# Last attention: odd heads' scores in the general banks, and one quarter of the down products a head

## The chip, the cores and the metric

One core of a Trainium2 chip runs the whole program. The metric is device time in microseconds (us), the median of several executions. TensorE does the matmuls, VectorE and ScalarE read and write PSUM (8 banks of 128 x 512 float32), GpSimd works on SBUF only, and SyncE issues the DMAs.

## The reference

The program is one transformer layer on x of 8 batches x 512 tokens x 512 features, in float32:

```python
x = x + _layernorm(attn(_layernorm(x), w_attn, b_attn, w_proj, b_proj))
x = x + _layernorm(ffn(_layernorm(x), w_fc, w_proj))

# attn: 16 heads of 32 features, rotary factors by head index
q, k, v = split(x @ w_attn + b_attn)
attn = softmax(where(causal, q @ k.T, -inf), axis=-1) * E ** -0.5
return (attn @ v) @ w_proj + b_proj
# ffn: both layers have ternary weights sign(round(w / mean|w|)) * mean|w|
# and a layer norm on their input (512 -> 2048 -> 512)
return bitlinear(gelu(bitlinear(x, w_fc)), w_proj)
```

## The kernel before

The work is staged as a software pipeline over the batches. Iteration `j` does the feed-forward part of batch j-1 (`prev`), the attention of batch j (`here`) and the projections to queries, keys and values of batch j+1 (`nxt`). With 8 batches the iterations run from -1 to 8, and iteration 7 is the one in which `prev` and `here` hold and `nxt` does not: the last attention. Iteration 8 has only the feed-forward part of batch 7. Each engine's program is written out by hand in order, with semaphores between them; there is no scheduler.

A float32 value is carried as a pair of float16 values, high and low. ScalarE writes the high half (`HI`) from a PSUM bank and leaves the whole value there, and VectorE subtracts the two (`low`, L950) to get the low half (`LO`). So every bank passes TensorE, ScalarE and VectorE before it is free.

The 8 PSUM banks are three `score` banks, three `gen` banks (general), `pv` and `down`. The general banks are handed out in a fixed order (`general_plan`), each use waiting for the third use before it to be drained (`claim`, semaphore `g_drained`); the score banks have a list of their own (`score_plan`, `claim_score`, `s_drained`). A head's scores fill three banks in parts of 512, 512 and 256 columns (`SCORE_W`).

After the 16 `up` products (L488) with their GELU, an iteration goes through its head loop. For head h TensorE issues the quarters of the down products that `DOWN_AT` lists for h (`ffn_down`, L531, 8 matmuls a quarter, 4 quarters for each tile of 128 tokens), then `scores(h + 1)` (a mask matmul, L563, and seven products, L557), then `weigh(h)`, the 20 products of probabilities and values (L585), which waits for all three subtractions of head h and for `pv` to be read out. In head 0 the quarter comes behind `weigh(0)`. The four quarters of tile 0 are done before the loop. ScalarE takes the exponentials of head h+1 (two per part, L809 and L811), and in heads 6, 9 and 13 a final normalisation of a tile (`FINISH_AT`, L816). VectorE subtracts for head h+1 (`probs_low`, L950), then reads out head h (`head_output`: reciprocal L1199, reduction L1201, product into xo L1206); in the heads of `FINAL_AT` it also drains the bank `down` of a tile (`final`, L1151) ahead of the subtractions and takes the moments (`final_moments`, L1157) behind them, and in head 6 the variance of the hidden layer, which waits for that head's weighing. GpSimd sums the squares of the hidden layer in the meantime (L1446, L1448, L1451), and head 6's `square_sums` on TensorE (L519) needs its last add. SyncE issues the stores of finished tiles, and in this iteration, behind the store of tile 2 and the last quarter, the load of the residual (L407).

Of the kernel before, what the change touches and what calls it, by code (L numbers as in the profile page):

```python
# [26 lines left out]
BATCHES, T, E, HEADS = 8, 512, 512, 16  # L27
HD = E // HEADS
F = 4 * E
PARTS = 128  # L30
# [10 lines left out]
S_UP = W_UP * W_UP  # L41
# [20 lines left out]
           13: [(3, 0), (3, 1)], 14: [(3, 2), (3, 3)]}  # L62
FINAL_AT = {8: 1, 12: 2}
SQUARES_AT = 6
FINISH_AT = {6: 0, 9: 1, 13: 2}
# [18 lines left out]


def general_plan(prev, here, nxt, setup):

    uses = []
    for u in range(FC):
        uses += [("shift", 0)] if here and u == SHIFT_AT else []  # L90
        uses += [("up", u)] if prev else []
        uses += [("xT", X_AT[u])] if nxt and u in X_AT else []
    if nxt and not here:
        uses += [("v", tb) for tb in range(TB)]
    for h in range(HEADS):
        uses += [("qk", QK_AT[h])] if nxt and h in QK_AT else []
        uses += [("next max", 3 * STEP_MAX[h] + i) for i in range(3)] if here and nxt and h in STEP_MAX else []
    if here:
        for name, n in (("v", 0), ("oT", 0), ("oT", 1), ("oT", 2), ("oT", 3), ("v", 1), ("x2T", 0), ("v", 2), ("x2T", 1), ("v", 3),
                        ("x2T", 2), ("x2T", 3)):  # L100
            if name != "v" or nxt:
                uses.append((name, n))
    return {name: k for k, name in enumerate(uses)}
# [9 lines left out]
def score_plan(here, nxt):  # L113

    uses = [("max", h) for h in range(EARLY, HEADS)] + [("scores", 0)] if here else []
    for h in range(HEADS):
        if here and h + 1 < HEADS:
            uses.append(("scores", h + 1))
    if nxt and not here:
        uses += [("next max", h) for h in range(EARLY)]  # L120
    return {use: 3 * k for k, use in enumerate(uses)}
# [31 lines left out]
def build(nc, x, w_attn, b_attn, b_v, w_proj, b_proj, w_fc, w_down, rope, out):  # L153
# [4 lines left out]
    HI, LO = 0, 1  # L158
# [4 lines left out]
    with ExitStack() as ctx:  # L163
# [256 lines left out]
        def _(pe):  # L420
# [41 lines left out]
            def iteration(j, prev, here, nxt, setup):  # L462
# [91 lines left out]
                def scores(h):  # L554
# [4 lines left out]
                    if h == 0:  # L559
                        pe.wait_ge(k_rows, 16)  # L560
                        pe.wait_ge(shift_rows, 32 * (j + 1))
                    bank = claim_score(("scores", h), 0)
                    nc.tensor.matmul(bank[:, :].rearrange("p (b t) -> p b t", b=TB), identb[:, :],  # L563
                                     mask_b[:, :].unsqueeze(1).to_broadcast([PARTS, TB, PARTS]),
                                     start=True, stop=False, skip_group_check=True)
                    for s in range(TB):
                        mm = part(bank, PARTS * s, s, PARTS * s, PARTS * (s + 1), False)
                    mm.then_inc(s_full, 1)
                    bank = claim_score(("scores", h), 1)
                    part(bank, 0, 0, PARTS, T, True)  # L570
                    part(bank, 384, 2, 3 * PARTS, T, False).then_inc(s_full, 1)
                    bank = claim_score(("scores", h), 2)
                    part(bank, 0, 1, 2 * PARTS, T, True).then_inc(s_full, 1)

                def weigh(h):

                    pe.wait_ge(s_drained, s0 + S["scores", h] + 3)
                    need(pe, pv_drained, HEADS * j + h)
# [44 lines left out]
                def project(tb):  # L623
# [3 lines left out]
                    if tb < 3:  # L627
                        pe.wait_ge(s_drained, s0 + S["scores", HEADS - 1] + tb + 1)
                    else:
                        pe.wait_ge(pv_drained, HEADS * (j + 1))  # L630
# [53 lines left out]
                for h in range(HEADS):  # L684
# [8 lines left out]
                    if nxt and not here and h == 5:  # L693
                        value_bias_projected()
                    pieces = DOWN_AT.get(h, ()) if prev else ()
                    if h:
# [51 lines left out]
        def _(act):  # L748
# [6 lines left out]
            def iteration(j, prev, here, nxt, setup):  # L755
# [49 lines left out]
                def exponents(h):  # L805

                    for i, n in enumerate(SCORE_W):
                        act.wait_ge(s_full, s0 + S["scores", h] + i + 1)
                        nc.scalar.activation(probs[:, h % 2, HI, 512 * i:512 * i + n], score[i][:, 0:n], ACT.Exp,  # L809
                                             scale=1.0 / S_UP)  # L810
                        nc.scalar.activation(score[i][:, 0:n], score[i][:, 0:n], ACT.Exp, scale=1.0 / S_UP  # L811
                                             ).then_inc(exp_full, 1)
# [132 lines left out]
        def _(dve):  # L945
# [69 lines left out]
            def iteration(j, prev, here, nxt, setup):  # L1015
# [170 lines left out]
                def probs_low(h):  # L1186

                    for i, n in enumerate(SCORE_W):
                        dve.wait_ge(exp_full, 48 * j + 3 * h + i + 1)
                        at = 512 * i  # L1190
                        low(probs[:, h % 2, LO, at:at + n], score[i][:, 0:n], probs[:, h % 2, HI, at:at + n]
                            ).then_inc(s_drained, 1)

# [78 lines left out]
                if nxt and not here:  # L1272
# [13 lines left out]
                    v_low(TB - 1)  # L1286
                    bias_ready()
                for h in range(HEADS):
                    if setup and h == 2:
# [9 lines left out]
                    if nxt and not here and h == 6:  # L1299
                        projection_bias()  # L1300
                    if prev and h in FINAL_AT:
                        final(FINAL_AT[h])
                    if prev and here and h == SQUARES_AT:
                        hidden_variance()
                        final_terms(0)
                    if here:
# [4 lines left out]
                        head_output(h)  # L1311
                    if prev and h in FINAL_AT:
                        final_moments(FINAL_AT[h])
                        final_terms(FINAL_AT[h])
                    if setup and h == 2:
# [214 lines left out]
```

## Time and profile before

| | us |
|---|---|
| median of 3 runs (range) | 1337.46 (1334.47 to 1338.87) |
| the profiled execution: its time | 1333.62 |
| its span, first to last instruction | 1331.8 |
| TensorE matmuls busy in the span | 1192.1 (90%) |
| VectorE / ScalarE / GpSimd busy | 1019.6 / 769.0 / 593.6 |
| last attention's head loop | 1165.2 to 1230.7 |

"Busy" counts the time of an engine's own operations; PE is TensorE's matmul, PEld its weight load, DVE is VectorE, ACT ScalarE, POOL GpSimd, SPq SyncE's DMA queue. "Idle before" and the name behind the arrow in brackets say how long an engine waited ahead of an operation and what ended the wait. PEclk is the clock granted to TensorE, 1.00 for 2.4 GHz and 0.50 for 1.2 GHz. Successive operations of one engine overlap in the records, so a pace is read from start to start. L12 is line 12 of the kernel. Head h of the last attention is known by its place: scores of head 0 stand ahead of the loop, those of head 1 at 1168.76 us.

### The profile page before, as it was taken

The numbers are of one execution on the slowest core, as the hardware profiler recorded it, in microseconds if no ns is written. First come the engines' busy times: TensorE is split into PE (matmuls) and PEld (weight loads), VectorE is DVE, ScalarE is ACT, GpSimd is POOL, SyncE is SP. The second block draws the span as 40 slices with busy tenths as digits, with TensorE's granted clock in tenths as the row PEclk, the third lists the DMA queues.
The fourth block names the chain that finished last, engine by engine and source line by source line (L and its number), as shares of the span: only waits on it lengthen the run. The fifth ranks groups of instructions, "written<-read, shape, count | busy, mean of one in ns | idle before, by whom it ended". The sixth has DMA issues, their size and how long they took to land.

```text
span 1331.8 us, 24946 instructions
## 1 busy us (share of the span) xinstructions
PE 1192.1 (90%) x9364; PEld 648.4 (49%) x9364; DVE 1019.6 (77%) x2931; ACT 769.0 (58%) x1414; POOL 593.6 (45%) x636
## 2 busy tenths in 40 slices
PE   4755879999999999999999999999999999988796
PEld 2322545455545554455545554455545554554352
DVE  7588896878878797978788787968787887776532
ACT  3334874666556664666556754666466755576470
POOL 6131441692049502791159412871259313971252
PEclk9865898999999999999999999999999999999798
DMA  5451122002310113002300213002300221001000
GB/s 205 132 154 62 38 70 57 1 2 57 96 40 3 39 51 103 1 8 67 89 32 2 57 43 94 1 18 70 106 1 3 57 78 27 2 9 48 9 1 32
DMA packets 49825, 65.37 MB, mean 49 GB/s; under 512 B 8581, under 2 KB 33189, under 8 KB 49192
## 3 DMA queue, kind: packets, MB, share of 16 engines
q1 hardware_dynamic: 49704, 63.77, 16.5%
q8 instruction: 74, 1.21, 0.4%
q14 instruction: 47, 0.39, 0.1%
HBM read 29.89 MB, written 8.39 MB: 29 GB/s over the span
## 4 chain that ended last, share of the span: by engine, by line
PE 51%; DVE 33%; ACT 8%; POOL 3%; issue 3%; SPq 1%; DMA 1%; POOLq 0%; DVEq 0%; ACTq 0%
PE gen L488 18%; PE down L531 17%; DVE score L1089 9%; PE pv L585 4%; DVE hT L950 4%; PE score L557 4%; DVE probs L950 2%; DVE acc_add L1066 2%; PE score L563 2%; DVE mx L1089 1%; DVE qkn L1181 1%; POOL rstd L1422 1%; DVE bn L1118 1%; ACT qkn L753 1%; PE gen L548 1%
## 5 line engine op out<-in xcount | busy, mean ns | idle before, releaser
L1422 POOL TENSOR_TENSOR rstd<-veps,mhalf 128x1 f32<-128x1 f32 (+1 forms) x104 | 67.5, 649 | 472.5 <-DVE veps L1166 363.9
L809 ACT ACTIVATE probs<-score 128x512 f16<-128x512 f32 (+1 forms) x384 | 202.4, 527 | 122.1 <-PE score L557 122.1
L950 DVE TENSOR_TENSOR probs<-score,probs 128x512 f16<-128x512 f32 (+1 forms) x384 | 213.4, 597 | 61.2 <-ACT score L811 60.8
L488 PE MATMUL gen<-x2T,t1T 128*128 128x512 f16 x1024 | 242.6, 382 | 4.0 <-ACT x2T L752 2.5
L531 PE MATMUL down<-t2T,hT 128*128 128x512 f16 x1024 | 234.1, 381 | 3.5 <-DVE xn L1151 3.5
L811 ACT ACTIVATE score<-score 128x512 f32<-128x512 f32 (+1 forms) x384 | 205.4, 535 | 0.0
L488 PE MATMUL gen<-xT,wa 128*128 128x512 f16 x768 | 178.6, 383 | 12.2 <-DVE wa L970 8.4
L950 DVE TENSOR_TENSOR hT<-gen,hT 128x512 f16<-128x512 f32 x160 | 108.9, 687 | 65.8 <-ACT gen L772 27.6
L1089 DVE CUSTOM_DVE_ANT_0 score<-score,mask_rows 128x512 f32<-128x512 f32 (+1 forms) x344 | 158.0, 523 | 0.0
L531 PEld LDWEIGHTS down<-t2T,hT 128*128 128x128 f16 x1024 | 96.7, 98 | 111.3 <-DVE xn L1151 4.7
L488 PEld LDWEIGHTS gen<-x2T,t1T 128*128 128x128 f16 x1024 | 95.4, 98 | 109.4 <-ACT x2T L752 5.2
L771 ACT ACTIVATE hT<-gen,gam 128x512 f16<-128x512 f32 x128 | 88.3, 690 | 95.5 <-PE gen L488 95.4
L1451 POOL TENSOR_TENSOR acc<-acc,acc_add 128x512 f32<-128x512 f32 x105 | 133.1, 1268 | 8.2
L1446 POOL TENSOR_TENSOR acc_add<-hT 128x512 f32<-128x512 f16 x105 | 121.3, 1155 | 14.8 <-POOL acc L1451 0.9
L488 PEld LDWEIGHTS gen<-xT,wa 128*128 128x128 f16 x768 | 72.1, 99 | 94.9 <-DVE wa L970 8.9
L1448 POOL TENSOR_TENSOR acc_add<-acc_add 128x512 f32<-128x512 f32 x105 | 109.4, 1041 | 8.2
L585 PE MATMUL pv<-v_sb,probs 128*128 128x65 f16 x2560 | 101.8, 196 | 5.5 <-DVE oA L1201 5.5
L585 PEld LDWEIGHTS pv<-v_sb,probs 128*128 128x128 f16 x2560 | 96.2, 99 | 12.5 <-DVE probs L950 6.9
L557 PE MATMUL score<-qk 98*128 98x128 f16 (+2 forms) x896 | 98.3, 247 | 1.4 <-DVE probs L950 1.4
L488 PE MATMUL gen<-wa,xT 128*128 128x512 f16 x384 | 90.3, 387 | 3.8 <-DVE wa L976 3.8
L753 ACT ACTIVATE qkn<-gen,qk_bias 128x512 f16<-128x512 f32 x64 | 44.1, 689 | 83.8 <-PE gen L488 73.7
L557 PEld LDWEIGHTS score<-qk 98*128 98x128 f16 x896 | 68.2, 99 | 43.0 <-DVE probs L950 7.0
(136 smaller groups left out, 1838.3 us busy)
## 6 DMA issues: line engine op xcount, KB each, us to landing
qk<-qkn SPq DMA_DIRECT2D x384, 64.0 KB, 2.0
xo<-x SPq DMA_DIRECT2D x8, 1024.0 KB, 5.6
hT<-x SPq DMA_DIRECT2D x8, 1024.0 KB, 6.3
out<-xn SPq DMA_DIRECT2D x32, 256.0 KB, 2.2
hT<-w_fc SPq DMA_DIRECT2D x4, 1024.0 KB, 6.4
hT<-w_down SPq DMA_DIRECT2D x4, 1024.0 KB, 5.5
hT<-w_attn SPq DMA_DIRECT2D x4, 512.0 KB, 10.0
hT<-w_attn SPq DMA_DIRECT2D x1, 1024.0 KB, 8.7
```

The lines of the kernel that those rows point to most:

```text
L488: mm = nc.tensor.matmul(bank[:, :], a, b, start=(start and n == 0), stop=(stop and n == len(pairs) - 1))
L531: mm = nc.tensor.matmul(down[:, :], hT[:, half, u, PARTS * tb:PARTS * (tb + 1)], t2T[:, u, :], start=(u == 0 and half == HI), stop=(u == F ...
L557: return nc.tensor.matmul(bank[:, at:at + t1 - t0], qk[0:98, 1, h, PARTS * s:PARTS * (s + 1)], qk[0:98, 0, h, t0:t1], start=start, stop=Tr ...
L585: mm = nc.tensor.matmul(pv[:, VW * tb:VW * (tb + 1)], probs[:, h % 2, half, at:at + PARTS], v_sb[:, s, h, :], start=(s == 0 and half == HI ...
L771: nc.scalar.activation(hT[:, HI, u, :], bank[:, :], ACT.Gelu, scale=gam[:, 0:1])
L809: nc.scalar.activation(probs[:, h % 2, HI, 512 * i:512 * i + n], score[i][:, 0:n], ACT.Exp, scale=1.0 / S_UP)
L811: nc.scalar.activation(score[i][:, 0:n], score[i][:, 0:n], ACT.Exp, scale=1.0 / S_UP).then_inc(exp_full, 1)
L950: return V.tensor_tensor(out, whole, hi, ALU.subtract)
L1089: op = V.tensor_tensor_reduce(part, part, mask_rows[:, T - n:T], 1.0, -3.0e38, ALU.add, ALU.max, mx[:, TB * u + tb:TB * u + tb + 1])
L1446: P.tensor_tensor(whole[:, :], hT[:, HI, u, :], hT[:, LO, u, :], ALU.add).then_inc(sq_step, 1)
L1448: P.tensor_tensor(whole[:, :], whole[:, :], whole[:, :], ALU.mult).then_inc(sq_step, 1 if u else 2)
L1451: P.tensor_tensor(acc[:, :], acc[:, :], acc_add[:, :], ALU.add).then_inc(sq_step, 1)
```

## The change

In the iteration without `nxt` the scores of odd heads go to the general banks (`scores_in_general`): the general plan gets three more uses for each odd head, the score plan loses them, and the waits and signals of TensorE, ScalarE and VectorE follow. The quarters of tiles 1 to 3 move from pairs in few heads to one in each of the heads 0, 1, 2, 4, 7, 8, 9, 10, 12, 13, 14 and 15 (`LAST_DOWN_AT`), and VectorE's finals of tiles 1 and 2 from heads 8 and 12 to heads 6 and 11. ScalarE's `FINISH_AT` stays. All other iterations are as they were.

```diff
 DOWN_AT = {0: [(1, 0)], 5: [(1, 1), (1, 2)], 6: [(1, 3)], 9: [(2, 0), (2, 1)], 10: [(2, 2), (2, 3)],
            13: [(3, 0), (3, 1)], 14: [(3, 2), (3, 3)]}
 FINAL_AT = {8: 1, 12: 2}
+LAST_DOWN_AT = {h: [divmod(n + 4, 4)] for n, h in enumerate((0, 1, 2, 4, 7, 8, 9, 10, 12, 13, 14, 15))}
+LAST_FINAL_AT = {6: 1, 11: 2}
...
+def scores_in_general(h, nxt):
+    return not nxt and h % 2 == 1 and h < HEADS
...
     for h in range(HEADS):
...
+        uses += [("scores", 3 * (h + 1) + i) for i in range(3)] if here and not nxt and scores_in_general(h + 1, nxt) else []
...
-        if here and h + 1 < HEADS:
+        if here and h + 1 < HEADS and not scores_in_general(h + 1, nxt):
             uses.append(("scores", h + 1))
...
+                    in_general = scores_in_general(h, nxt)
+                    full = g_full if in_general else s_full
+                    def claim_part(i):
+                        return claim("scores", 3 * h + i) if in_general else claim_score(("scores", h), i)
-                    bank = claim_score(("scores", h), 0)
+                    bank = claim_part(0)
...
-                    pe.wait_ge(s_drained, s0 + S["scores", h] + 3)
+                    if scores_in_general(h, nxt):
+                        drained("scores", 3 * h + 2)
+                    else:
+                        pe.wait_ge(s_drained, s0 + S["scores", h] + 3)
...
-                        pe.wait_ge(s_drained, s0 + S["scores", HEADS - 1] + tb + 1)
+                        pe.wait_ge(s_drained, s0 + S["scores", HEADS - 1 if nxt else HEADS - 2] + tb + 1)
...
-                    pieces = DOWN_AT.get(h, ()) if prev else ()
+                    pieces = (DOWN_AT if nxt or not here else LAST_DOWN_AT).get(h, ()) if prev else ()
...
-                        act.wait_ge(s_full, s0 + S["scores", h] + i + 1)
+                        if scores_in_general(h, nxt):
+                            bank = filled("scores", 3 * h + i)
+                        else:
+                            act.wait_ge(s_full, s0 + S["scores", h] + i + 1)
+                            bank = score[i]
...
-                        low(probs[:, h % 2, LO, at:at + n], score[i][:, 0:n], probs[:, h % 2, HI, at:at + n]
-                            ).then_inc(s_drained, 1)
+                        bank = bank_of("scores", 3 * h + i) if in_general else score[i]
+                        low(probs[:, h % 2, LO, at:at + n], bank[:, 0:n], probs[:, h % 2, HI, at:at + n]
+                            ).then_inc(g_drained if in_general else s_drained, 1)
...
+                final_at = FINAL_AT if nxt or not here else LAST_FINAL_AT
...
-                    if prev and h in FINAL_AT:
-                        final(FINAL_AT[h])
+                    if prev and h in final_at:
+                        final(final_at[h])
```

On TensorE, heads 4 and 5 of the last attention, before, from the weighing of head 3 to the scores of head 6:

```order
L585 MATMUL pv<-v_sb,probs 128x65 x20
L563 MATMUL score<-mask_b,identb 128x512
L557 MATMUL score<-qk 128x128 x4
L557 MATMUL score<-qk 128x384
L557 MATMUL score<-qk 128x128
L557 MATMUL score<-qk 128x256
L585 MATMUL pv<-v_sb,probs 128x65 x20
L531 MATMUL down<-t2T,hT 128x512 x16
L563 MATMUL score<-mask_b,identb 128x512
```

The same place after the change (the lines of the kernel have moved by 8 to 17):

```order
L602 MATMUL pv<-v_sb,probs 128x65 x20
L539 MATMUL down<-t2T,hT 128x512 x8
L577 MATMUL gen<-mask_b,identb 128x512
L565 MATMUL gen<-qk 128x128 x4
L565 MATMUL gen<-qk 128x384
L565 MATMUL gen<-qk 128x128
L565 MATMUL gen<-qk 128x256
L602 MATMUL pv<-v_sb,probs 128x65 x20
L577 MATMUL score<-mask_b,identb 128x512
```

The two quarters (16 matmuls) between the weighing of head 4 and the scores of head 6 are gone from there, one quarter (8) stands ahead of the scores of head 5, and those scores are in the general banks.

At the end of the loop on TensorE, before, from the scores of head 14 on:

```order
L563 MATMUL score<-mask_b,identb 128x512
L557 MATMUL score<-qk 128x128 x4
L557 MATMUL score<-qk 128x384
L557 MATMUL score<-qk 128x128
L557 MATMUL score<-qk 128x256
L585 MATMUL pv<-v_sb,probs 128x65 x20
L531 MATMUL down<-t2T,hT 128x512 x16
L563 MATMUL score<-mask_b,identb 128x512
L557 MATMUL score<-qk 128x128 x4
L557 MATMUL score<-qk 128x384
L557 MATMUL score<-qk 128x128
L557 MATMUL score<-qk 128x256
```

After that the old program has the weighings of heads 14 and 15 in one row (`x40`). The new one, from the scores of head 15 on:

```order
L577 MATMUL gen<-mask_b,identb 128x512
L565 MATMUL gen<-qk 128x128 x4
L565 MATMUL gen<-qk 128x384
L565 MATMUL gen<-qk 128x128
L565 MATMUL gen<-qk 128x256
L602 MATMUL pv<-v_sb,probs 128x65 x20
L539 MATMUL down<-t2T,hT 128x512 x8
L602 MATMUL pv<-v_sb,probs 128x65 x20
```

The last quarter has moved in between the weighings of heads 14 and 15.

On VectorE in head 6, from the output of head 5 on, before:

```order
L1206 TENSOR_TENSOR xo<-oA,r_sum 128x4x32
L1138 TENSOR_TENSOR h_msq<-h_negm 128x4
L1140 SCALAR_TENSOR_TENSOR h_var<-pv,h_msq 128x4
L1143 TENSOR_SCALAR e_fin<-h_var,c_fin 128x4
L1166 TENSOR_TENSOR veps<-mv,e_fin 128x1
L950 TENSOR_TENSOR probs<-score,probs 128x512 x2
```

And now:

```order
L1229 TENSOR_TENSOR xo<-oA,r_sum 128x4x32
L1172 SCALAR_TENSOR_TENSOR xn<-c_sum,h_negm,down 128x512
L1159 TENSOR_TENSOR h_msq<-h_negm 128x4
L1161 SCALAR_TENSOR_TENSOR h_var<-pv,h_msq 128x4
L1164 TENSOR_SCALAR e_fin<-h_var,c_fin 128x4
L1187 TENSOR_TENSOR veps<-mv,e_fin 128x1
L971 TENSOR_TENSOR probs<-gen,probs 128x512 x2
```

The final of tile 1 (`xn<-c_sum,h_negm,down`) now stands ahead of the variance, and its moments follow behind the output of head 6.

## Rows read from the trace of the kernel before

**Rows 1.** view in windows of the head loop; first line names the columns
```profile
core 0: us, PE busy (x) PEld busy (x) DVE busy (x) ACT busy (x) POOL busy (x), PEclk, DMA share, GB/s
...
1165.20:1230.70 65.50, 53.67 (x564) 32.30 (x562) 47.59 (x114) 44.64 (x99) 27.73 (x28) 0.95 0.09 29
...
1172.50:1181.30 8.80, 5.74 (x84) 3.51 (x82) 7.85 (x18) 7.84 (x19) 8.06 (x8) 1.00 0.01 2
...
1190.00:1193.90 3.90, 2.22 (x35) 1.75 (x32) 2.30 (x10) 2.67 (x6) 0.55 (x1) 0.97 0.00 0
...
1187.10:1204.20 17.10, 14.96 (x146) 9.70 (x145) 12.61 (x33) 11.45 (x25) 4.28 (x7) 0.80 0.05 17
```

**Rows 2.** waits in the head loop: us in total, times, longest
```profile
ACT probs L809 <- PE score L557: 18.7, 11, 3.4
```

**Rows 3.** timeline of ScalarE: start us, us, engine, line, out<-in, idle before
```profile
1169.40 0.60 ACT L809 ACTIVATE probs<-score 128x512 f16<-128x512 f32 x1 [1.56 <-PE score L557]
...
1172.50 0.60 ACT L809 ACTIVATE probs<-score 128x512 f16<-128x512 f32 x1 [0.44 <-PE score L557]
...
1175.08 0.61 ACT L809 ACTIVATE probs<-score 128x512 f16<-128x512 f32 x1
...
1187.09 0.60 ACT L809 ACTIVATE probs<-score 128x512 f16<-128x512 f32 x1 [3.13 <-PE score L557]
...
1222.97 0.81 ACT L816 ACTIVATE xn<-xn,shift,rstd 128x512 f32<-128x512 f32 x1
...
1225.22 0.60 ACT L809 ACTIVATE probs<-score 128x512 f16<-128x512 f32 x1 [1.44 <-PE score L557]
```

**Rows 4.** timeline of TensorE, heads 0 to 2
```profile
1168.76 0.38 PE L563 MATMUL score<-mask_b,identb 128*128 128x512 bf16 x1
...
1169.53 0.77 PE L585 MATMUL pv<-v_sb,probs 128*128 128x65 f16 x20
...
1170.13 1.89 PE L531 MATMUL down<-t2T,hT 128*128 128x512 f16 x8
...
1171.86 0.38 PE L563 MATMUL score<-mask_b,identb 128*128 128x512 bf16 x1
...
1174.37 0.39 PE L563 MATMUL score<-mask_b,identb 128*128 128x512 bf16 x1 [0.51 <-DVE probs L950]
```

**Rows 5.** timeline of VectorE and TensorE at the last head
```profile
1227.35 1.02 DVE L950 TENSOR_TENSOR probs<-score,probs 128x512 f16<-128x512 f32 x2 [0.31 <-ACT score L811]
...
1228.91 0.78 PE L585 MATMUL pv<-v_sb,probs 128*128 128x65 f16 x20 [2.80 <-DVE oA L1201]
```

**Rows 6.** timeline of VectorE: the product of a head, beside GpSimd and alone
```profile
1176.15 1.25 DVE L1206 TENSOR_TENSOR xo<-oA,r_sum 128x128 f32<-128x128 f32 x1
...
1182.35 0.29 DVE L1206 TENSOR_TENSOR xo<-oA,r_sum 128x128 f32<-128x128 f32 x1
```

**Rows 7.** timeline: weighing of heads 6 and 7, statistics of tile 1
```profile
1191.62 0.76 PE L585 MATMUL pv<-v_sb,probs 128*128 128x65 f16 x20
...
1195.36 1.31 PE L585 MATMUL pv<-v_sb,probs 128*128 128x65 f16 x20
...
1202.07 0.68 DVE L1157 BATCH_NORM_STATS2 bn<-xn 128x6 f32<-128x512 f32 x1
```

**Rows 8.** timeline of TensorE: weighing of head 12, then tile 3's first quarters
```profile
1215.32 0.76 PE L585 MATMUL pv<-v_sb,probs 128*128 128x65 f16 x20 [0.21 <-DVE oA L1201]
...
1216.29 3.63 PE L531 MATMUL down<-t2T,hT 128*128 128x512 f16 x16 [0.21 <-DVE xn L1151]
```

**Rows 9.** timeline of GpSimd: its last sum of squares
```profile
1187.44 1.27 POOL L1451 TENSOR_TENSOR acc<-acc,acc_add 128x512 f32<-128x512 f32 x1
```

**Rows 10.** timeline of TensorE: products of the first and the second projection
```profile
1232.37 3.89 PE L488 MATMUL score<-wp,hT 128*128 128x512 f16 x12
...
1236.74 2.75 PE L488 MATMUL score<-wp,hT 128*128 128x512 f16 x12
```

**Rows 11.** DMA issues of the page: KB each, median us to landing
```profile
hT<-x SPq DMA_DIRECT2D x8, 1024.0 KB, 6.3
```

More of the change, by code:

```diff
@@ L567, in scores @@
                         mm = part(bank, PARTS * s, s, PARTS * s, PARTS * (s + 1), False)
-                    mm.then_inc(s_full, 1)
-                    bank = claim_score(("scores", h), 1)
+                    mm.then_inc(full, 1)
+                    bank = claim_part(1)
                     part(bank, 0, 0, PARTS, T, True)
-                    part(bank, 384, 2, 3 * PARTS, T, False).then_inc(s_full, 1)
-                    bank = claim_score(("scores", h), 2)
-                    part(bank, 0, 1, 2 * PARTS, T, True).then_inc(s_full, 1)
+                    part(bank, 384, 2, 3 * PARTS, T, False).then_inc(full, 1)
+                    bank = claim_part(2)
+                    part(bank, 0, 1, 2 * PARTS, T, True).then_inc(full, 1)
                 def weigh(h):
-                    pe.wait_ge(s_drained, s0 + S["scores", h] + 3)
+                    if scores_in_general(h, nxt):
+                        drained("scores", 3 * h + 2)
+                    else:
+                        pe.wait_ge(s_drained, s0 + S["scores", h] + 3)
                     need(pe, pv_drained, HEADS * j + h)
@@ L807, in exponents @@
                     for i, n in enumerate(SCORE_W):
-                        act.wait_ge(s_full, s0 + S["scores", h] + i + 1)
-                        nc.scalar.activation(probs[:, h % 2, HI, 512 * i:512 * i + n], score[i][:, 0:n], ACT.Exp,
+                        if scores_in_general(h, nxt):
[3 more added lines that the diff above has]
+                            bank = score[i]
+                        nc.scalar.activation(probs[:, h % 2, HI, 512 * i:512 * i + n], bank[:, 0:n], ACT.Exp,
                                              scale=1.0 / S_UP)
-                        nc.scalar.activation(score[i][:, 0:n], score[i][:, 0:n], ACT.Exp, scale=1.0 / S_UP
+                        nc.scalar.activation(bank[:, 0:n], bank[:, 0:n], ACT.Exp, scale=1.0 / S_UP
                                              ).then_inc(exp_full, 1)
@@ L1190, in probs_low @@
                         at = 512 * i
-                        low(probs[:, h % 2, LO, at:at + n], score[i][:, 0:n], probs[:, h % 2, HI, at:at + n]
-                            ).then_inc(s_drained, 1)
+                        in_general = scores_in_general(h, nxt)
+                        bank = bank_of("scores", 3 * h + i) if in_general else score[i]
+                        low(probs[:, h % 2, LO, at:at + n], bank[:, 0:n], probs[:, h % 2, HI, at:at + n]
+                            ).then_inc(g_drained if in_general else s_drained, 1)
                 def head_output(h):
@@ L1311, in iteration @@
                         head_output(h)
-                    if prev and h in FINAL_AT:
-                        final_moments(FINAL_AT[h])
-                        final_terms(FINAL_AT[h])
+                    if prev and h in final_at:
+                        final_moments(final_at[h])
+                        final_terms(final_at[h])
                     if setup and h == 2:
```

## The prediction

> **What bounds the kernel now.** I read the page first, then the stretch of the last attention in windows, the list of waits there, the chain of waits, and the timeline of that stretch engine by engine. Nothing before 1165 us changes, since both edits are switched by "no next batch", so only the 65.5 us of the last attention's head loop [rows 1] and what follows it can move. In that stretch TensorE is busy 53.67 us, VectorE 47.59, ScalarE 44.64: none is full, so it is a question of how they wait for each other. The longest sum of waits on the working engines is ScalarE's for score matmuls, 18.7 us [rows 2].
>
> The reader is to see three paces there. I call M(h) the start of head h's mask matmul, E(h) the start of its first exponential, W(h) the start of its weighing matmuls. (a) ScalarE's own pace: E(2) to E(3) is 1172.50 to 1175.08, 2.58 us a head with no wait between [rows 3]. (b) TensorE's pace with one down quarter in the head: M(1) at 1168.76, W(0) at 1169.53, the quarter at 1170.13, M(2) at 1171.86 [rows 4]: 0.77 + 0.60 + 1.73 = 3.10. (c) Two quarters in one head make it 3.10 + 1.73 = 4.83, and ScalarE then stands idle: 3.13 us ahead of E(6) at 1187.09 [rows 3]. So the heads without a quarter run at ScalarE's pace while TensorE idles (5.74 of 8.80 us busy in 1172.5 to 1181.3 [rows 1]), and those with two at TensorE's pace while ScalarE idles. The 14 head gaps from E(1) at 1169.40 to E(15) at 1225.22 make 55.8; at ScalarE's pace they would be 14 x 2.58 + 3 finals x 0.8 [rows 3] = 38.5. The other 17.3 and the 1.56 ahead of E(1) are the 18.7 of [rows 2].
>
> **The change part by part.** Work: the same matmuls, exponentials and subtractions, on other banks and in another order. Nothing is added or removed but waits.
>
> The spread of the quarters is the term that pays. The constants for the new order come from rows: M to E 0.64 (1168.76 to 1169.40 [rows 3, 4]); M to W at least 0.77, W to the next matmul 0.60, a quarter 1.73 [rows 4]; E to W 3.69 where nothing else stands on VectorE (1225.22 to 1228.91, the three subtractions and then the reduction of the head before [rows 3, 5]); a final on ScalarE 0.8 [rows 3]. In the new order M(h+1) follows W(h-1) + 0.60 + the quarter; a wait for a bank is never last, because head h+1 uses the banks of head h-1, whose subtractions end before W(h-1) begins. So M(h+1) = W(h-1) + 0.60 + 1.73 q; E(h) = the later of M(h) + 0.64 and E(h-1) + 2.58; W(h) = the later of E(h) + 3.69 and M(h+1) + 0.77. Up to W(0) = 1169.53 and E(1) = 1169.40 nothing moves (M(1) waits for the last half of tile 0, not for a bank).
>
> Head by head, in us after 1165: two quarters lie between W(0) and M(2) (those of heads 0 and 1): M(2) 8.6, E(2) 9.2, W(1) 9.4. Quarter of head 2: M(3) 11.7, E(3) 12.3, W(2) 12.9. None: M(4) 13.5, E(4) 14.9, W(3) 16.0. Quarter: M(5) 18.4, E(5) 19.0, W(4) 19.1. Two heads with none: E(6) 21.6, W(5) 22.7, M(7) 23.3, E(7) 24.2, W(6) 25.3. Here sits a detour that stays: the variance waits for head 6's weighing, and W(7) comes 3.74 after W(6) (1191.62 to 1195.36 [rows 7]); new W(7) = 29.0. M(8) 27.6, and ScalarE's final of tile 0 holds E(8) to 28.6. VectorE's moments of tile 1, now done ahead of head 8's subtractions, cost some 1.3 (0.68 for the statistics [rows 7], and three short steps), on top of a 1.25 product, so W(8) is 33.3 and not 32.3. Then four quarters in a row: M(9) 31.4, E(9) 32.0; M(10) 35.7, E(10) 36.3, W(9) 36.5; M(11) 38.8, E(11) 39.7 behind a final, W(10) 40.0; M(12) 40.6, E(12) 42.3, W(11) 43.4. Tile 3's first quarter waits for the final on VectorE, which starts after head 10's output: it started 0.97 after a weighing (1215.32 to 1216.29 [rows 8]) and does so again, at 44.4: M(13) 46.1, E(13) 46.7, W(12) 46.9. M(14) 49.2, E(14) 49.8, W(13) 50.4; M(15) 52.8, E(15) 53.4, W(14) 53.5; W(15) = E(15) + 3.69 = 57.1. The last quarter, now in head 15, ends at 53.5 + 2.33 = 55.8, so it is hidden by 1.3 us behind that wait; without the cover it would cost 1.73. Before, W(15) was at 63.9 [rows 5]. Gain 6.8.
>
> The banks by themselves: in the old scheme M(h+1) also waits for head h's first subtraction, E(h) + 1.87 (1172.50 to M(3) at 1174.37 [rows 3, 4]), and with M to E 0.64 that gives E(h+1) = E(h) + 2.51, no more than ScalarE's own 2.58. So they pay only where VectorE is late with that subtraction: after a slow product (below), at the variance, and at the finals in heads 6 and 11. I put 1 to 2 of the 6.8 on them, and nothing on the fixed cost of another bank, since the same engines read general banks of the same size all through the kernel; from the nearest rows this is 0 on both sides.
>
> What I subtract: VectorE's product of a head takes 0.29 us, but 1.25 where GpSimd's sum of squares runs beside it [rows 6]. GpSimd works without a break until 1188.71 [rows 9], so heads 1 to 6 meet it. Of the five such products before it ended, one paid the full 0.96 and the others 0 to 0.3, mean about 0.3; they delay W only where E + 3.69 decides, heads 2, 3, 5 and 6. Bounds 0 and 4 x 0.96 = 3.8; I take 0.8, nearer the low end, because most of the observed ones were short. The specification table of the Trainium skill's "GPSIMD Engine Reference" ("Specifications") says that GpSimd shares its SBUF interfaces with VectorE, with contention for instructions with two SBUF inputs. By that rule every such product could pay, and the sum would go to the 3.8 end, a gain of 3.0; the rows show the 1.25 once in five, so the trace agrees on the mechanism and not on its being always paid.
>
> The squares' sums ahead of W(6) need GpSimd's last add. New, they can start at 24.2 (M(7) + 0.77 + 0.16), and that add ended at 23.7 [rows 9]: covered by 0.5 us only. If GpSimd is a microsecond later, 0.5 is lost there.
>
> The tail (from W(15) on) moves as it is. The residual's load waits for the last quarter, which now ends at 55.8, that is 1220.8, and lands 6.3 later [rows 11], at 1227.1. Its first reader comes behind the first projection, 1236.3 before [rows 10] and 1229.5 or later now, so it stays hidden, by 2.4 us at least. The clock of TensorE is the unknown. It was at 1.00 (2.4 GHz) in heads 2 to 5, and fell to the other level (1.2 GHz) behind a stretch with 2.22 of 3.90 us busy: a mean of 0.80 over 17.10 us means 6.8 us at half speed [rows 1]. It fell again for the first projection, whose 12 matmuls took 3.89 against 2.75 in the next [rows 10]. My sum takes full speed in the loop and the same tail. Bounds: if the tail's fall goes, +1.1; if a fall lands on the four quarters in a row, as long a one, 6.8 us, costs at most the 3.4 us of full-speed work that doesn't fit into it.
>
> Sum: 6.8 - 0.8 = 6.0 us. Against the profiled execution, 1333.62 (span 1331.8), that is 1327.6. The median of the three runs is 1337.46, 3.8 above the profiled one, so the forecast for the median is 1337.46 - 6.0 = 1331.5.
>
> **The rivals.** First, the clock falls in the new order as well and meets heads 7 to 10, which all hold a quarter. For it: heads 5 and 6 have no quarter and my times give TensorE 0.77 + 0.60 + 0.77 + 1.02 = 3.2 of 5.6 us, the same share as where it fell. Against: the quarters around them are fuller than before. Price 3.4: gain 2.6, 1334.9.
> Second, the shared port: each of the four products pays 0.96. For it [rows 6], against it the other four of five. Gain 6.8 - 3.8 = 3.0, 1334.5.
> Third, larger: no fall in the loop and none at the first projection, since TensorE now idles 1.3 us and not 2.8 ahead of W(15) [rows 5]; the slow-port loss also stays out. Gain 6.8 + 1.1 = 7.9, 1329.6.
> Fourth, slower: the clock falls twice in the loop (after heads 3 to 4 and after 5 to 6) and stays low into the start of the last up products. Against it: the old order had a sparser stretch, 1172.5 to 1181.3, at full clock throughout [rows 1]. Each fall costs up to 3.4, three of them 10.2, against a gain of 6.0: 1341.7. It decides from the second fall on, at which the gain is used up.
> That the change does not do what it says would be a second bank set that still waits for the first. It can't here: each wait for a general bank is three uses back, which is the same part of the head two before. What can be empty is its use, as the 2.51 against 2.58 above says, and that is in the sum.
>
> **How the numbers follow.** Forecast 0.55, clock on the quarters 0.17, port 0.09, larger 0.12, slower 0.07. A difference under 0.3%, 4.0 us, can't be told from no change in this kernel. Of the forecast's 0.55, whose own range is a gain of 4 to 8, I give 0.51 to above 4.0 and 0.04 below; the larger case adds 0.12: faster 0.63. The two small gains and the 0.04 make same 0.30, slower 0.07. The range leaves out the slower case and the far end of the larger: gain 0.5 to 9.5 with the runs' own scatter of some 2 us inside, 1328 to 1337.
>
> **What would show it.** E(15) about 49 us after E(1) in place of 55.8; no ScalarE wait for scores over 1.5 us after head 2 (3.13 and more before); W(h) to W(h+2) about 6.7 in the run of heads 8 to 10; the last quarter over before W(15); the granted clock at 1.00 through the loop; and W(15) near 1222. Wrong would be: W to W+2 longer than 7, GpSimd the one waited for at the squares' sums, or a loop shorter by 6 while the tail is longer by as much.

## The result and the profile after

| | before | after |
|---|---|---|
| median, 5 runs each (range), us | 1337.46 (1334.47 to 1339.36) | 1329.26 (1326.26 to 1331.13) |
| ratio, with its 95% interval | | 0.9937 (0.9915 to 0.9959) |
| profiled execution, its time / span | 1333.62 / 1331.8 | 1331.13 / 1329.3 |

Compared twice more, against new runs of before, the changed kernel stood at 0.9958 (0.9945 to 0.9971) and 0.9921 (0.9908 to 0.9935). So the gain is 5.6, 8.2 and 10.6 us in the three comparisons, where 6.0 was forecast.

The one profile shows 2.5 us of it. Splitting it at two points, the first mask matmul of the loop (head 0) and the last weighing, says why. The first rows are TensorE's timeline in the changed kernel: start us, us, engine, line, operation, and in brackets the idle time before it and what ended that.

```profile
1167.68 0.38 PE L577 MATMUL score<-mask_b,identb 128*128 128x512 bf16 x1
...
1172.67 0.77 PE L602 MATMUL pv<-v_sb,probs 128*128 128x65 f16 x20
...
1177.50 0.78 PE L602 MATMUL pv<-v_sb,probs 128*128 128x65 f16 x20
...
1181.06 0.76 PE L602 MATMUL pv<-v_sb,probs 128*128 128x65 f16 x20 [0.28 <-DVE oA L1224]
...
1184.17 1.18 PE L602 MATMUL pv<-v_sb,probs 128*128 128x65 f16 x20 [1.58 <-DVE oA L1224]
1185.16 3.15 PE L539 MATMUL down<-t2T,hT 128*128 128x512 f16 x8
...
1197.78 3.60 PE L539 MATMUL down<-t2T,hT 128*128 128x512 f16 x8
...
1215.54 0.77 PE L602 MATMUL pv<-v_sb,probs 128*128 128x65 f16 x20 [1.75 <-DVE oA L1224]
1216.50 1.90 PE L539 MATMUL down<-t2T,hT 128*128 128x512 f16 x8 [0.20 <-DVE xn L1172]
...
1226.27 1.89 PE L539 MATMUL down<-t2T,hT 128*128 128x512 f16 x8
1229.23 0.78 PE L602 MATMUL pv<-v_sb,probs 128*128 128x65 f16 x20 [1.06 <-DVE oA L1224]
...
1232.33 2.76 PE L496 MATMUL score<-wp,hT 128*128 128x512 f16 x12
```

The reader is to see four things. The loop starts at 1167.68, 3.1 us later than before (1164.54), in a part that is the same in both kernels. The weighings of heads 0 to 3 stand 5.0, 9.8, 13.4 and 16.5 us behind that start. Then two quarters take 3.15 and 3.60 us where the others take 1.9: TensorE was at the lower level of its clock (1.2 GHz) for most of each. And the last weighing comes 61.5 us after the start, 64.4 before ([rows 5], from 1164.54). The last quarter starts 2.96 us ahead of it and so is hidden, as said. Across the loop and at the two quarters, the windows say the same (time, then busy us of each engine, then PEclk):

```profile
1167.70:1229.20 61.50, 52.77 (x553) 32.21 (x550) 47.09 (x112) 44.39 (x99) 28.09 (x29) 0.92 0.04 14
```

```profile
1184.00:1188.00 4.00, 3.83 (x28) 2.06 (x29) 3.63 (x8) 1.72 (x5) 3.60 (x4) 0.57 0.00 0
1194.00:1201.50 7.50, 6.50 (x39) 4.15 (x39) 5.14 (x16) 3.42 (x8) 1.59 (x3) 0.54 0.00 0
```

ScalarE's waits for scores, in the list of waits of the changed kernel's loop, are two rows now, since odd heads read general banks:

```profile
ACT probs L830 <- PE gen L565: 7.5, 6, 3.1
ACT probs L830 <- PE score L565: 6.8, 5, 2.2
```

That is 14.3 us against 18.7 [rows 2]. Both hold the wait ahead of head 0's exponentials, 1.96 and 1.95 us; without it they are 12.3 and 16.7. Its timeline shows where the 3.1 is: behind the slow quarter of head 4. Further on the longest is 1.79 us.

```profile
1188.79 0.60 ACT L830 ACTIVATE probs<-gen 128x512 f16<-128x512 f32 x1 [3.07 <-PE gen L565]
...
1205.03 0.60 ACT L830 ACTIVATE probs<-gen 128x512 f16<-128x512 f32 x1 [0.45 <-PE gen L565]
...
1218.88 0.60 ACT L830 ACTIVATE probs<-gen 128x512 f16<-128x512 f32 x1 [1.79 <-PE gen L565]
...
1225.54 0.60 ACT L830 ACTIVATE probs<-gen 128x512 f16<-128x512 f32 x1 [0.18 <-PE gen L565]
```

From 1172.54 to 1225.54, E(1) to E(15) is 53.0 us, against 55.8 before and 49 forecast.

### The profile page after: what moved, and what is told of

Read it like the earlier page. It is cut to its first block, busy times and chain, and to the rows that moved or that the text cites. A ratio compares the mean times of both kernels' runs of the same rounds, so it can differ in the third digit from the quotient of the medians.

```text
span 1329.3 us, 24946 instructions
## 1 busy us (share of the span) xinstructions
PE 1192.4 (90%) x9364; PEld 649.2 (49%) x9364; DVE 1019.6 (77%) x2931; ACT 767.0 (58%) x1414; POOL 593.1 (45%) x636
## 4 chain that ended last, share of the span: by engine, by line
PE 50%; DVE 33%; ACT 9%; issue 3%; POOL 3%; SPq 1%; DMA 1%; POOLq 0%; DVEq 0%; ACTq 0%
PE gen L496 18%; PE down L539 16%; DVE score L1110 9%; PE pv L602 4%; DVE hT L971 4%; PE score L565 4%; DVE probs L971 2%; DVE acc_add L1087 2%; POOL rstd L1446 1%; DVE bn L1139 1%; PE score L577 1%; DVE mx L1110 1%; DVE qkn L1202 1%; ACT probs L830 1%; PE gen L556 1%
## 5 line engine op out<-in xcount | busy, mean ns | idle before, releaser
L830 ACT ACTIVATE probs<-score 128x512 f16<-128x512 f32 x360 | 189.5, 526 | 110.7 <-PE score L565 110.7
L971 DVE TENSOR_TENSOR probs<-score,probs 128x512 f16<-128x512 f32 x360 | 199.8, 596 | 53.2 <-ACT score L832 52.6
L832 ACT ACTIVATE score<-score 128x512 f32<-128x512 f32 x360 | 192.3, 534 | 0.0
L602 PE MATMUL pv<-v_sb,probs 128*128 128x65 f16 x2560 | 101.8, 196 | 9.4 <-DVE oA L1224 9.4
L602 PEld LDWEIGHTS pv<-v_sb,probs 128*128 128x128 f16 x2560 | 96.2, 99 | 17.6 <-DVE probs L971 13.4
L565 PE MATMUL score<-qk 98*128 98x128 f16 x840 | 90.2, 247 | 0.0
L1484 POOL TENSOR_SCALAR acc<-hT,theta 128x512 f16<-128x512 f32 x24 | 41.6, 1738 | 101.4 <-DVE g_sq L1063 76.2
```

The lines of the kernel that those rows point to most:

```text
L565: return nc.tensor.matmul(bank[:, at:at + t1 - t0], qk[0:98, 1, h, PARTS * s:PARTS * (s + 1)], qk[0:98, 0, h, t0:t1], start=start, stop=Tr ...
L602: mm = nc.tensor.matmul(pv[:, VW * tb:VW * (tb + 1)], probs[:, h % 2, half, at:at + PARTS], v_sb[:, s, h, :], start=(s == 0 and half == HI ...
L832: nc.scalar.activation(bank[:, 0:n], bank[:, 0:n], ACT.Exp, scale=1.0 / S_UP).then_inc(exp_full, 1)
L971: return V.tensor_tensor(out, whole, hi, ALU.subtract)
```

## The experiments

Each kernel with a ratio was compared with runs of before on the same chip at the same time; kernels measured together against the same runs of before are called a series. One series holds the banks alone, the spread alone, the changed kernel's second profile and the quarters in 0, 2, 4, 5; another holds the third profile and the last two kernels of the table; a third holds the old banks with those quarters, the short squares and the masks for 4, 6, 12. "Loop" is from head 0's mask matmul to the last weighing, "tail" from there to the end of the span, "start" the time of that mask matmul, all of the one profiled execution. Before and the spread alone were profiled once more and the changed kernel twice more, because one execution doesn't show how the clock falls in others.

| kernel | ratio (95%) | start | loop | clock in the loop | tail |
|---|---|---|---|---|---|
| before | 1 | 1164.5 | 64.4 | 0.95 | 102.9 |
| before, again | | 1167.6 | 65.2 | 0.92 | 102.0 |
| changed | 0.9937 (0.9915 to 0.9959) | 1167.7 | 61.5 | 0.92 | 100.1 |
| changed, second | 0.9958 (0.9945 to 0.9971) | 1165.8 | 61.6 | 0.92 | 101.2 |
| changed, third | 0.9921 (0.9908 to 0.9935) | 1164.2 | 60.5 | 0.94 | 100.2 |
| banks only | 0.9986 (0.9973 to 0.9998) | 1165.0 | 65.2 | 0.92 | 101.3 |
| spread only | 0.9946 (0.9931 to 0.9961) | 1164.3 | 58.7 | 1.00 | 101.9 |
| spread only, again | | 1164.8 | 58.7 | 1.00 | 101.8 |
| quarters 0, 2, 4, 5 | 0.9936 (0.9923 to 0.9949) | 1166.4 | 60.9 | 0.94 | 100.1 |
| the same, old banks | 0.9947 (0.9927 to 0.9967) | 1166.6 | 60.8 | 0.94 | 100.0 |
| changed, short squares | 0.9963 (0.9950 to 0.9976) | 1166.5 | 61.3 | 0.92 | 102.8 |
| changed, masks repeated for 4, 6, 12 | 0.9933 (0.9915 to 0.9951) | 1166.6 | 60.5 | 0.94 | 100.2 |
| changed, masks repeated for 7, 12 | 0.9926 (0.9913 to 0.9939) | 1168.1 | 59.9 | 0.97 | 101.8 |
| quarters 0, 2, 4, 5, masks for 4, 12 | 0.9914 (0.9901 to 0.9927) | 1165.2 | 57.9 | 0.97 | 103.0 |

**The banks alone.**

```diff
-LAST_DOWN_AT = {h: [divmod(n + 4, 4)] for n, h in enumerate((0, 1, 2, 4, 7, ...))}
-LAST_FINAL_AT = {6: 1, 11: 2}
+LAST_DOWN_AT = DOWN_AT
+LAST_FINAL_AT = FINAL_AT
```

> Only the banks change: odd heads' scores in the general banks, quarters and finals in their old heads. Theory A (the spread of the quarters pays, the banks hardly): by the rule of the prediction the old wait for a score bank allows a head every 2.51 us, under ScalarE's 2.58, so only VectorE's late subtractions are relieved: a gain of 0 to 2 us on before, with 3.1 us of ScalarE idle still ahead of heads 6 and 14. Theory B (the old bank wait was the stall): most of the change's 8 us is here, a gain of 6 to 8 us, and the spread alone brings under 2.

Measured: 0.9986, 1.9 us less than before, with its loop at 65.2 us. Theory B falls; the banks by themselves are worth 0.3 to 3.6 us by the interval, as theory A said. The loop of that profile is not shorter than before's. Its weighings run 0.5 to 0.6 us ahead of before's first profile from head 4 to head 8, but then two pairs of quarters take 4.49 and 4.46 us, where before's first profile has 4.00 and 3.63, because the clock was low for longer there. So the loop shows a small lead and not a gain.

**The spread alone.**

```diff
 def scores_in_general(h, nxt):
-    return not nxt and h % 2 == 1 and h < HEADS
+    return False
```

TensorE's wait for the last score banks behind the loop goes back to the one of before with it.

> Only the quarters and finals move; all scores stay in the score banks. Theory A: a gain of 5 to 8 us on before; the loop from head 0's mask matmul to the last weighing is 57 to 59 us where the clock stays up, against 64.4 before. Theory B: the spread quarters can't be used while every head waits for the bank of the head before: a gain under 2 us.

Measured: 0.9946, 7.2 us less, and loops of 58.7 us. That is all of the change's gain within the intervals; the changed kernel in the same series had 0.9958, so putting the general banks on top of the spread added nothing that can be seen. The row over the loop has the clock at 1.00:

```profile
1164.30:1223.00 58.70, 50.95 (x554) 29.90 (x551) 47.64 (x112) 44.50 (x99) 28.08 (x29) 1.00 0.04 15
```

> The kernel with only the quarters moved, once more, for its profile. Its first profile had no fall of the clock in the loop and 58.7 us from head 0's mask matmul to the last weighing. Theory C with falls that depend on where the execution stands: the loop is again 58.7 us if the clock stays up, and 60 to 63 us with one or two falls. If the order of work alone decided, it is 58.7 again.

It was the same to 0.01 us, with the clock up throughout, from a start 0.6 us later. Two starts so near each other don't tell whether the order alone decides or the start too. Both profiles are of quick executions, 1326.7 and 1327.2 us, where this kernel's timed runs go from 1326.1 to 1330.7; whether the clock falls in the loop of the longer ones is not known.

**The changed kernel again, and a third time.**

> The changed kernel itself, for one more profile of its loop. If the two falls of the clock seen in its first profile (15 us into the loop and 28 us into it) belong to the order of work, they are there again and the loop is 61 to 62 us. If they depend on where the execution happens to stand, they come elsewhere or not at all, and a loop without them is 57.6 us from head 0's mask matmul to the last weighing, as the prediction's head by head list has it. Time 1326 to 1332 us.

> The changed kernel a third time, on the chip of the two kernels with repeats, to compare with. Its falls at 26 and 46.5 us into the loop again (61.6 us), unless the loop starts elsewhere, as in the first profile, where they were at 16.6 and 26.9. Time 1327 to 1331 us.

The second profile had falls 26 and 46.5 us behind the start, and 61.6 us; the third, from the start of 1164.2, had only the one at 26, and 60.5; the first, above, had them at 16.6 and 27. So the third expectation was half right: no fall at 46.5, and a median just below the expected range (1326.75). Where the clock fell changed with the start of the loop within one order; that it fell in this order was so in all three.

**No two heads in a row without a quarter.**

```diff
-... enumerate((0, 1, 2, 4, 7, 8, 9, 10, 12, 13, 14, 15))}
+... enumerate((0, 2, 4, 5, 7, 8, 9, 10, 12, 13, 14, 15))}
```

> As the changed kernel, but tile 1's quarters in heads 0, 2, 4 and 5 and not 0, 1, 2 and 4: no two heads in a row without a quarter, and no double one ahead of head 2's scores. By the prediction's rules this is 0.8 us shorter at full clock. If sparse stretches in heads 3 and 5 to 6 are what lowers TensorE's clock, the falls become rarer and it gains 1 to 4 us on the changed kernel; if the falls don't follow the sparse heads, the two differ by under 1 us.

> All scores in the score banks, tile 1's quarters in heads 0, 2, 4 and 5. If the old bank wait costs next to nothing beside the spread (theory A), the same as the run with these heads and the general banks, 1327 us within 1.5. If the banks pay once no head pair is empty, 2 us or more slower than that.

Measured 0.9936 and, with old banks, 0.9947; loops of 60.9 and 60.8, both with falls 16 and 46.5 us behind the start and none at 26. The fall behind heads 5 and 6 went when head 5 got a quarter. Another came at 16, behind heads 1 and 3, of which head 1 had its quarter taken away. The start isn't the reason: the changed order with short squares starts at 1166.5 as well and has no fall at 16. With these heads the banks make no difference in the loop, as theory A has it; the ratios are 1.5 us apart, inside their intervals. Beside the 0.9936 the changed kernel had 0.9958, 2.9 us more, but 0.9937 and 0.9921 in its other two comparisons, so this order is not shown to be faster.

**Repeated mask matmuls.** The mask matmul starts the sum in its bank (start=True). Here it is issued several times into the same bank ahead of the scores; the extra ones change nothing in the result and only keep TensorE at work.

```diff
+                    for _ in range({4: 4, 6: 6, 12: 6}.get(h, 1) if not nxt else 1):
                         nc.tensor.matmul(bank[:, :]..., identb[:, :], mask_b..., start=True, stop=False, ...)
```

> The changed kernel with its mask matmul repeated into the same bank where TensorE has nothing else to do: 4 times for head 4, 6 times for heads 6 and 12 (each 0.216 us, start=True, so the result is the same). It adds 0.65 to 1.1 us of TensorE work to three sparse heads, inside slack by the prediction's rules (0.7, 1.2 and 1.2 us). Theory C (a sparse TensorE lowers the clock and that costs the loop 3 to 4 us): fewer falls in the loop, 1 to 4 us faster than the changed kernel. Rival (the falls don't depend on these heads): the same falls, 0 to 1 us slower.

The fall at 46.5 was gone, the one at 26 stayed, and the loop was 60.5: the third changed profile has the same without any repeats, from a start 2.3 us earlier. More telling are the three profiles without repeats for head 12 whose loops start within 0.2 us of this one's 1166.56: short squares and quarters 0, 2, 4, 5 with either banks. All three fell at 46.5, their quarters there taking 3.06, 3.54 and 3.56 us, and this one took 1.90. That is in favour of theory C, with one profile on its side. The time was 0.9933.

The next kernel has `{7: 4, 12: 6}` there.

> The changed kernel with the mask matmul repeated 4 times for head 7 and 6 times for head 12. With repeats for heads 4, 6 and 12 the fall at 46.5 us was gone and the one at 26 stayed. Theory C: head 7's scores stand right ahead of that fall, so it goes as well, and the loop is 58 to 59.5 us (0.5 us of the repeats can't be hidden there). Rival: the fall at 26 us belongs to the squares' sums and stays, the loop is 60.5 to 61.

Its loop started at 1168.1, near that of the first profile of the changed kernel (1167.7), which fell at 16.6 and at 27. It fell at 16.6 too, and not at 27. TensorE's timeline of that place, first of that profile of the changed kernel, then of this one:

```profile
1192.48 0.77 PE L602 MATMUL pv<-v_sb,probs 128*128 128x65 f16 x20 [2.03 <-DVE oA L1224]
1193.08 0.38 PE L577 MATMUL gen<-mask_b,identb 128*128 128x512 bf16 x1
1193.30 0.71 PE L565 MATMUL gen<-qk 98*128 98x128 f16 x7
1195.01 1.84 PE L527 MATMUL pv<-ones,acc 128*128 128x1 f32 x8 [1.00 <-DVE probs L971]
1196.71 1.26 PE L602 MATMUL pv<-v_sb,probs 128*128 128x65 f16 x20
1197.78 3.60 PE L539 MATMUL down<-t2T,hT 128*128 128x512 f16 x8
```

```profile
1192.89 0.77 PE L603 MATMUL pv<-v_sb,probs 128*128 128x65 f16 x20 [2.03 <-DVE oA L1225]
1193.50 1.02 PE L578 MATMUL gen<-mask_b,identb 128*128 128x512 bf16 x4
1194.36 0.71 PE L565 MATMUL gen<-qk 98*128 98x128 f16 x7
1195.43 1.02 PE L527 MATMUL pv<-ones,acc 128*128 128x1 f32 x8 [0.35 <-issue]
1196.31 0.76 PE L603 MATMUL pv<-v_sb,probs 128*128 128x65 f16 x20
1196.91 1.89 PE L539 MATMUL down<-t2T,hT 128*128 128x512 f16 x8
```

Three more mask matmuls in head 7, 0.65 us of work, and the squares' sums take 1.02 and not 1.84, the quarter 1.89 and not 3.60. All five profiles of this order without repeats for head 7 fell here, this one didn't, so theory C is supported for this fall, again by one profile. In time nothing is gained: 0.9926 beside 0.9921 for the changed kernel in the same series.

**Quarters in 0, 2, 4, 5 and masks repeated for heads 4 and 12.**

> General banks for odd heads, tile 1's quarters in heads 0, 2, 4 and 5, and the mask matmul repeated 6 times for heads 4 and 12, ahead of the two places where the clock fell in that order (15.8 and 46.5 us behind head 0's mask matmul). Theory C (sparse TensorE work lowers the clock, and work laid in there keeps it up): no fall in the loop, 57 to 58 us from head 0's mask matmul to the last weighing in place of 60.9, and 1 to 3 us faster than the same order without the repeats. Rival (falls come where they like): one or two falls at other places, no gain.

The loop was 57.9, as expected, though the clock did fall once, briefly, at 26, which was not expected. The falls at 16 and 46.5 were gone, but the loop started 1.3 us earlier than that of the same order without repeats, so what removed them is not shown. With 0.9914 it is the fastest kernel of the study, and it beats before by 11.5 us; its interval overlaps those of the other two kernels of its series, so against the changed kernel (0.9921) it is not shown to be faster. The tail was 103.0: against the changed kernel's third profile the loop is 2.6 us shorter and the tail 2.8 us longer, so in these two profiles the one makes up for the other.

**GpSimd's sums of squares shortened.** For all but the first of the 16 parts of the hidden layer, the three steps of the sum (the diff shows one) cover 8 of 512 columns in this iteration, so the squares of the other columns are left out of the variance.

```diff
+                    c = slice(0, T) if nxt or not u else slice(0, 8)
...
-                    P.tensor_tensor(whole[:, :], hT[:, HI, u, :], hT[:, LO, u, :], ALU.add)
+                    P.tensor_tensor(whole[:, c], hT[:, HI, u, c], hT[:, LO, u, c], ALU.add)
...
```

> The changed kernel with GpSimd's sums of squares cut to 8 of 512 columns in the last attention's iteration and the one after the loop's start unchanged otherwise (tile sums of later columns are left out). Theory D (the shared port costs 0.8 us in this loop, the term of the prediction): VectorE's product takes 0.29 us in every head up to 6, the loop is 0.5 to 1.5 us shorter than the changed kernel's. Rival (it is worth up to 3.8): 3 us or more. If nothing waits for it, no difference.

GpSimd's busy time in the loop fell from 28.1 to 6.0 us, and every product of heads 0 to 5 took 0.29, where it had taken 0.56 to 1.40 in most of the first five. Three rows of VectorE's timeline, the products of heads 2, 3 and 4, first with short squares, then in the third profile of the changed kernel:

```profile
1182.95 0.29 DVE L1229 TENSOR_TENSOR xo<-oA,r_sum 128x128 f32<-128x128 f32 x1
1185.53 0.29 DVE L1229 TENSOR_TENSOR xo<-oA,r_sum 128x128 f32<-128x128 f32 x1
1189.61 0.29 DVE L1229 TENSOR_TENSOR xo<-oA,r_sum 128x128 f32<-128x128 f32 x1
```

```profile
1180.69 0.29 DVE L1229 TENSOR_TENSOR xo<-oA,r_sum 128x128 f32<-128x128 f32 x1
1183.27 1.40 DVE L1229 TENSOR_TENSOR xo<-oA,r_sum 128x128 f32<-128x128 f32 x1
1187.35 1.08 DVE L1229 TENSOR_TENSOR xo<-oA,r_sum 128x128 f32<-128x128 f32 x1
```

The loop was 61.3 against the 61.6 of the second changed profile, which has its falls at the same two places. So these products are slow because GpSimd works beside them, and little waits for it: the squares' sums on TensorE begin 0.5 us earlier (25.7 us behind the start and not 26.2), 0.3 us of which is left at the end of the loop, and there is no gain in time (0.9963). The products of heads 6, 9 and 13 still took 1.20 to 1.23 us, in this kernel as in the others; a GpSimd addition of 1.26 us for a finished tile ran beside each (1197.61 to the product's 1197.83 in head 6). The edit doesn't touch those, so what they cost is not measured.

**The kernel before, once more.**

> The kernel before once more, for a second profile to set beside three of the changed kernel. The medians of before in four calls were 1335.6 to 1338.3 us, and its profiled execution, 1333.6, was one of the fastest. If the gain in the timed runs is that of the loop and the tail (3 and 2 us in the profiles), this profile splits as 1164 to 1168 us ahead of head 0's mask matmul, 64 to 65 in the loop and 103 to 105 behind the last weighing. If the loop of before varies as much as the changed kernel's, it is 66 or more.

Start 1167.6, loop 65.2, tail 102.0, the last 1 us below what was expected. The start varies by 3 us in before too, and by 3.9 over all 14 profiles, ahead of anything that was changed. It goes with the clock of the setup: in 100 to 200 us its mean was 0.79 in before's first profile and the changed kernel's third (starts 1164.5 and 1164.2), and 0.75 in before's second and the changed kernel's first two (1165.8 to 1167.7).

## Why the prediction was right

**The mechanism.** The quarters next to each other were what cost time, the banks hardly: the spread alone gave 7.2 us and the banks alone 1.9 (0.3 to 3.6). "I put 1 to 2 of the 6.8 on them" fits the banks alone, but not the new order: with the spread in place they added nothing that was seen (0.9958 with them, 0.9946 without; with quarters in 0, 2, 4, 5 the loops are 60.9 and 60.8). One reading ahead of it is off: the 18.7 us of [rows 2] hold head 0's 1.95 at 1165.18, so 17.3 + 1.56 doesn't make them up; it comes near by chance.

**The signs.** Of those that the prediction named, two held in the changed kernel's first profile: W(8) to W(10) took 6.65 us for 6.7, and the last quarter was over before W(15). Four didn't: W(15) came at 1229.2 and not near 1222, 3.1 us of that by the later start, E(1) to E(15) took 53.0 us and not 49, ScalarE waited up to 3.07 us for scores behind head 2, and the clock was at 0.92 and not 1.00. In the profiles the loop gained 3.6 us of the 6.0 forecast and the tail, put at nothing, 2.0. That the sum came out near the forecast is so in part luck. The median is nearest the third rival, 1329.6, but of its two conditions (no fall in the loop, none at the first projection) only the second was met, and in two of three profiles.

**Head by head.** Up to W(3) the list holds to 0.1 us. The start was put 0.46 us ahead of the 1165 of the list, so its W(0) to W(3), 4.5, 9.4, 12.9 and 16.0, are 5.0, 9.9, 13.4 and 16.5 behind the start; measured 5.0, 9.8, 13.4, 16.5. The spread-only kernel keeps to the list's rhythm at full clock to the end, except for one step at W(6): 57.1 + 0.46 = 57.6 was forecast without contention, and 58.7 measured.

**What was missing: the squares' sums in series.** The forecast took W(6) as E(6) + 3.69 and let TensorE do the squares' sums in the gap ahead of it. In `weigh` the waits for head 6's subtractions and for `pv` stand ahead of them, so they start when the weighing could, and delay it. The cover I named (GpSimd's last add) was not the one that counted. These rows show it: the sums and the weighing in the spread-only profile, then the sums in the changed kernel's third profile, then with short squares.

```profile
1190.43 1.02 PE L527 MATMUL pv<-ones,acc 128*128 128x1 f32 x8 [0.16 <-issue]
1191.32 0.76 PE L602 MATMUL pv<-v_sb,probs 128*128 128x65 f16 x20
```

```profile
1190.47 1.83 PE L527 MATMUL pv<-ones,acc 128*128 128x1 f32 x8 [1.54 <-DVE probs L971]
```

```profile
1192.18 1.63 PE L527 MATMUL pv<-ones,acc 128*128 128x1 f32 x8 [1.00 <-DVE probs L971]
```

From each start (1164.27, 1164.24, 1166.50) the sums begin at 26.2, 26.2 and, with short squares, 25.7; the list has 25.8 for the weighing itself. The weighing follows 0.9 behind them at full clock. So W(6) came 27.05 behind the start, where 25.3 + 0.46 = 25.76 was forecast: 1.3 us later, 0.9 of it the sums, put at nothing, and the rest, 0.4 to 0.5, VectorE late behind a slow product of head 4 (1.02 and 1.08 us in place of 0.29). W(15) was 1.2 later, so that one step is all of it.

**The port: mis-sized.** 0.8 was subtracted for it; by the short squares it is 0.5 at head 6. With the 0.9 of the sums 1.3 was due. The two mistakes go opposite ways, and the loop at full clock came out 0.4 us longer than forecast.

**The clock: the larger term.** The sum took full speed in the loop. In all three changed profiles it fell, once or twice, and the loop was 1.8 to 2.9 us longer than the 58.7 of the spread alone, which had no fall. The first rival gave 3.4 for this, so its mechanism did happen, and a chance of 0.17 was too low for it. The first profile even has both falls of the fourth rival, behind heads 3 to 4 and 5 to 6; at up to 3.4 each they would have used up the gain, and the two together cost 2.8. It did not decide the time, because before falls too (64.4 and 65.2 us, one and two falls): from profiles, the loop gained 64.8 - 61.2 = 3.6 us on the mean.

**The tail: not "as it is".** It was 102.9 and 102.0 before and 100.1, 101.2 and 100.2 after, 2.0 us shorter on the mean. The third rival named one cause, the first projection at full clock: 2.76 in place of 3.89 [rows 10] in two of three profiles, 3.53 in the other; before's second profile has 3.63. The windows from the last weighing to the second group of up products put it at 1.2 us; here before's first profile, then the changed kernel's:

```profile
1228.90:1264.90 36.00, 27.66 (x137) 13.89 (x138) 20.33 (x54) 15.68 (x23) 8.63 (x19) 0.76 0.06 23
```

```profile
1229.20:1264.00 34.80, 25.00 (x137) 12.67 (x138) 20.16 (x54) 15.53 (x23) 8.62 (x19) 0.85 0.12 38
```

Another 1.6 us of the first pair is one down tile of 32 matmuls in the last iteration, 8.65 in before's first profile and 7.08 in its second and in all three of the changed kernel. It differs between two executions of before, so the change isn't needed to explain it; both spread-only profiles have it too (8.68 and 8.66), which is why their tails are 101.9 and 101.8 with the first projection at 2.76. Loop and tail together are 5.5 us in the profiles; the timed gain is 5.6, 8.2 and 10.6. The difference is within what the start, the falls and two to three profiles a side leave open, and is not settled.

## What to carry to other kernels

When a loop alternates between iterations bound by one engine and iterations bound by another, spread the filler work evenly before giving the loop more buffers: here the first alone gave 7.2 us, the second alone 1.9, and both together, measured beside them, 5.6. Write the recurrence of the loop from start-to-start times and then check each wait against the code line by line, since a step that stands behind a semaphore isn't in the gap that the timeline shows. And a saving in one stage must be priced with TensorE's clock in it, in several profiles: one profile of each kernel would have shown 2.5 us of a gain of 8.

## What the runs showed that was not expected

The granted clock is not only scatter: with nearly the same start (1164.2 to 1164.8) the spread-only order didn't fall in its two profiles and the changed one did in its one, though what the general banks change there is that the scores of heads 4, 6 and 7 run about 1 us sooner. I read it so that work done earlier leaves TensorE with longer unbroken waits (2.03 us ahead of head 5's weighing); that this is the cause was not shown by itself. In one profile 0.65 us of extra matmuls stood where a fall was gone. And across the timed runs of the changed kernel, those at a mean clock of 0.961 or more took 1326.0 to 1329.4 us and those at 0.957 or less 1330.5 to 1331.3: the scatter of this kernel goes with the clock.
